# First attention of a fused transformer kernel: the scores of four heads as four row tiles of TensorE, in one set of PSUM banks, the values one step behind

## The chip, the cores and the metric

One Trainium2 chip; the kernel runs on one of its cores. The metric is the device time of one launch in microseconds. "Engines" are TensorE (PE; its weight loads are shown apart as PEld), VectorE (DVE), ScalarE (ACT), GpSimd (POOL) and SyncE (SP, which starts the transfers). PSUM has 8 banks of 128 partitions by 512 float32.

## The reference, cut to what matters

```python
x = L0_attn_x                                     # (1, 2048, 128)
x = x + _L0_attn_ref(_layernorm(x), w_qkv, w_proj, q_norm_w, k_norm_w)   # the first attention
x = x + _L0_ffn_ref(_layernorm(x), ...)           # a linear map by way of an FFT
x = x + _L1_attn_ref(_layernorm(x), ...)          # a linear attention
x = x + _L1_ffn_ref(_layernorm(x), ...)           # the second attention, 8 heads of 64, experts
# _L0_attn_ref: 16 heads of 8, causal, 2048 tokens
qkv = (x @ w_qkv.T).reshape(1, 2048, 3, 16, 8).transpose(2, 0, 3, 1, 4)
q, k = rope(rms_norm(q, q_norm_w)), rope(rms_norm(k, k_norm_w))
attn = jnp.einsum('bhqd,bhkd->bhqk', q, k) * 8 ** -0.5
attn = softmax(jnp.where(causal, -jnp.inf, attn), axis=-1)
out = jnp.einsum('bhqk,bhkd->bhqd', attn, v) ... @ w_proj.T
```

The change touches the first attention alone.

## The kernel before, in words

The tokens are 16 tiles of 128 (P); four tiles are a chunk of 512 (CH), and there are four chunks (NC). The 16 heads go in four groups (NG) of four (GH). In a group each head owns 32 partitions: `qT` holds the queries of the four heads under one another, and `kM[g % 2][:, h, :]` holds the keys of head h on partitions 32h to 32h+31 and zeros elsewhere. A matmul over all 128 partitions with `kM[.., h, ..]` as weights so gives the scores of head h alone.

**Foreground.** For a group there are 40 steps `STEPS0`, (c, jt) with query chunk c and key tile jt from 0 to 4c+3; over the four groups that is 160 steps k. In 96 of them the key tile lies before the chunk (jt < 4c, "off the diagonal": 512 queries), in 64 it lies on the diagonal (width 512, 384, 256 and 128 in turn, `off = diag(c, jt)`, and a second matmul adds the causal mask). For each step:
- S: the scores of the four heads, keys on partitions, into PSUM banks 0 to 3. Before, a unit u is two heads of a step (u = 2k, 2k+1), in banks 0, 1 or 2, 3; the unit waits until ACT has read the unit two before (`s_exp`, NS = 2).
- ACT takes the exponential of two banks at a time into `pbuf0` (line 976), two instructions a step.
- V: four matmuls, one for each head, as four column tiles (32 columns of weights each) into bank 6 (line 734), summed over the key tiles of a chunk. They are float32, and the trace shows two passes for each (8 a step). Before, V(k) is issued two steps behind S.
- O: after the last V of a chunk ACT copies bank 6 to `oT`; F: PE transposes it, DVE divides and stores it.

**Background.** Between them the preparation of the following chunks and group is woven in: transposes "k", "q", "q2" (line 667; ACT copies them out, "k" by four instructions of 32 partitions, line 963, "q" and "q2" by one, line 967), and "max" steps, in which PE computes scores with the queries on partitions (line 700, mask line 704) and DVE takes their maximum (line 1201, or line 1198 with a mask). The maximum goes into "q2" so that the exponentials don't overflow. These steps, and F and the later "at", "pj", "lt", "mix", "lin", share a ring of three banks, `RING0 = (4, 5, 7)`: in `take`, a step waits until the step three before it in the ring has been read out of its bank.

**The order.** One list, `SEQ0`, is followed by each engine. `preparation0` and `paced` give every background step a place on a scale of units (80 to a group); `merge` goes through the half units and puts, ahead of each, the background steps whose place has come, then what `foreground0(u, half)` returns. Before: S(u) at half 0 of each unit, V(k) (and O) at half 1 of unit 2k+4, F at half 1 of unit 2k+9. `after0` places the work that follows the last group.

Of the kernel before, what the change touches and what calls it, by code (L numbers as in the profile page):

```python
# [26 lines left out]
ACT = mybir.ActivationFunctionType  # L27
AX = mybir.AxisListType

P = 128  # L30
# [3 lines left out]
CH = 512  # L34
NC = T // CH
TPC = CH // P
H0, D0 = 16, 8
GH = 4
NG = H0 // GH
# [5 lines left out]
NP0, NP1 = 6, 5  # L45
NS = 2
# [152 lines left out]
def build(nc, A):  # L199
    ctx = ExitStack()  # L200
    with ctx:
# [6 lines left out]
        ps = ctx.enter_context(nc.psum_tensor("ps", [P, 8, CH], F32))  # L208
# [28 lines left out]
        identr = sm("identr", [P, P], F32R)  # L237
        maskr = sm("maskr", [P, 2, P], F32R)
# [22 lines left out]
        qT = s0("qT", [P, 2, T], F32R)  # L261
# [8 lines left out]
        pbuf0 = s0("pbuf0", [P, NP0, 2, CH])  # L270
# [20 lines left out]
        kM = (kM0, kM1)  # L291
# [71 lines left out]
        s_sc = sem("s_sc")  # L363
        s_exp = sem("s_exp")
        s_av = sem("s_av")
# [39 lines left out]
        STEPS0 = [(c, jt) for c in range(NC) for jt in range(TPC * (c + 1))]  # L405
        N0 = len(STEPS0)
        LAST0 = [TPC * (c + 1) * (c + 2) // 2 for c in range(NC)]
# [2 lines left out]


        def foreground0(u, half):
            if half == 0:
                return [("S", u)] if u < 2 * N0 * NG else []
            seq = []
            k = u // 2 - 2
            if u % 2 == 0 and 0 <= k < N0 * NG:
                seq.append(("V", k))
                if k % N0 + 1 in LAST0:
                    seq.append(("O", k // N0, LAST0.index(k % N0 + 1)))  # L420
            k = u // 2 - 4
            if u % 2 and 0 <= k < N0 * NG and k % N0 + 1 in LAST0:
                seq.append(("F", k // N0, LAST0.index(k % N0 + 1)))
            return seq

# [17 lines left out]

        after0 = []
        for c in range(NC):
            u = 2 * (N0 * (NG - 1) + LAST0[c] + 3) + 1
            for i, kind in enumerate(("at", "pj", "sd", "ln", "lt", "mix", "sd2", "ln2", "lt2")):
                after0.append((u + 1.8 + 1.6 * i, (kind, c)))
                if c == NC - 1 and kind in ("sd", "sd2"):
                    after0 += [(u + 2.0 + 1.6 * i, ("kv", b)) for b in ((0,) if kind == "sd" else (1, 2))]  # L450
            u += 1.8 + 1.6 * 9
            i = 3 * c
            for a, step in enumerate((("lin", i), ("lin", i + 1), ("ex", i), ("el", i), ("lin", i + 2), ("ex", i + 1),
                                      ("el", i + 1), ("ex", i + 2), ("el", i + 2))):
                after0.append((u + 0.8 * a, step))
# [31 lines left out]
        def diag(c, jt):  # L487
            return max(0, P * (jt - TPC * c))
# [89 lines left out]
        def _(sp):  # L578
# [24 lines left out]
                r = min(P, E1 * D1 - P * i)  # L603
                sp.dma_start(wout[0:r, i, :], A["Wo"][P * i:P * i + r, :]).then_inc(s_load1, 16)
            sp.dma_start(fold[:], A["fold"]).then_inc(s_load1, 16)
            sp.wait_ge(s_sc, 2 * N0 * NG)
            for h in range(H1):
                if h:
                    sp.wait_ge(s_wh, 3 * h)
# [13 lines left out]
        def _(pe):  # L623
# [54 lines left out]
            for step in SEQ0:  # L678
# [27 lines left out]
                                       start=False, stop=True, skip_group_check=True)  # L706
                    mm.then_inc(s_turn0, 1)
                elif kind == "S":
                    u = step[1]
                    g, (c, jt) = u // (2 * N0), STEPS0[u // 2 % N0]  # L710
                    off = diag(c, jt)
                    if u >= NS:
                        pe.wait_ge(s_exp, u - NS + 1)
                    wait_read(pe, ring0, ("q2", g, c))
                    wait_read(pe, ring0, ("k", g, c))
                    for i in range(2):
                        h = 2 * (u % 2) + i
                        b = 2 * (u % NS) + i
                        mm = pe.matmul(ps[:, b, off:CH], kM[g % 2][:, h, P * jt:P * (jt + 1)],  # L719
                                       qT[:, g % 2, CH * c + off:CH * (c + 1)], start=True, stop=jt < TPC * c)  # L720
                        if jt >= TPC * c:
                            mm = pe.matmul(ps[:, b, off:off + P], identr[:], maskr[:, 1, :], start=False, stop=True)  # L722
                    mm.then_inc(s_sc, 1)
                elif kind == "V":
                    k = step[1]
# [201 lines left out]
        def _(act):  # L927
# [22 lines left out]
            for step in SEQ0:  # L950
                kind = step[0]
                if kind in ("k", "q", "q2"):
                    _, g, c = step
                    wait_turn(act, ring0, step)
                    if g >= 2:
                        act.wait_ge(s_sc, 2 * N0 * (g - 1))
                    b = ring0.bank(step)
                    if kind == "k":
                        if g == 1:
# [7 lines left out]
                        nc.scalar.activation(qT[:, g % 2, CH * c:CH * (c + 1)], ps[:, b, :],  # L967
                                             ACT.Copy).then_inc(s_read0a, 1)
                elif kind == "S":
                    u = step[1]  # L970
                    off = diag(*STEPS0[u // 2 % N0])
                    act.wait_ge(s_sc, u + 1)
                    if u >= NP0:
                        act.wait_ge(s_av, (u - NP0) // 2 + 1)
                    b = 2 * (u % NS)
                    nc.scalar.activation(pbuf0[:, u % NP0, :, off:CH], ps[:, b:b + 2, off:CH], ACT.Exp,  # L976
                                         scale=float(D0) ** -0.5).then_inc(s_exp, 1)
                elif kind == "O":
                    _, g, c = step
                    m = g * NC + c  # L980
# [119 lines left out]
        def _(dve):  # L1100
# [61 lines left out]
            for step in SEQ0:  # L1162
# [74 lines left out]
                elif kind == "lin":  # L1237
                    i = step[1]
                    wait_turn(dve, ring0, step)
                    if i == 0:  # L1240
                        dve.wait_ge(s_stagev, NG)
                        dve.wait_ge(s_sc, 2 * N0 * (NG - 1))
                        dve.wait_ge(s_load1, 16 * 16)
                        v.memset(vf[:, :, D:D + 1], 1.0)
                        v.memset(vf[:, :, D + 1:D + 2], 0.0)
# [359 lines left out]
```

## Time and profile before

| | us |
|---|---|
| median of 3 runs | 1695.55 |
| lowest, highest | 1686.46, 1697.53 |
| profiled execution | 1687.58 |
| its span | 1685.8 |
| first attention in it, first to last step | 75.5 to 606.8 |

The profile comes from one execution. Busy times of PE are partly modelled (a matmul's end); starts are more reliable, so stretches on PE are read from start to start. An idle time in brackets stands before the instruction, with what ended it.

### The profile page before, as it was taken

What the parts mean: (1) busy time and instruction counts of PE and PEld (TensorE: products, weight loads), DVE (VectorE), ACT (ScalarE), POOL (GpSimd) and SP (SyncE); (2) the same over time, 40 slices, a digit from 0 to 9 for tenths busy, and PEclk for the clock granted to TensorE, in tenths of its full rate; (3) what the DMA queues carried; (4) which work ended last, traced back from release to release, by engine and by line L of the source; (5) the groups of instructions that cost most, each with busy time, mean ns of one, the idle gap of its engine ahead of it and who ended that gap; (6) DMA issues with size and microseconds to landing.
All of it is one profiled execution on the core that took longest, in us unless ns stands there. A gap on an engine that the chain in (4) does not pass through costs nothing.

```text
span 1685.8 us, 27140 instructions
## 1 busy us (share of the span) xinstructions
PE 1556.2 (92%) x8404; PEld 1012.7 (60%) x8404; DVE 1254.2 (74%) x2518; ACT 939.7 (56%) x1582; POOL 847.9 (50%) x935
## 2 busy tenths in 40 slices
PE   4699999999999976689999999999999999999998
PEld 2455565565565545466666666567576666666555
DVE  3997787687679536777887778787778787777664
ACT  3446756756755631344655655655655656556652
POOL 2530000000001133458869879788689699698452
PEclk9599999999999987989999999999999999999998
DMA  2000000000000000000000000000000000000000
GB/s 64 0 1 1 2 1 2 1 1 1 1 1 1 1 12 13 1 1 13 0 13 1 1 13 2 0 13 1 13 1 1 13 1 1 1 1 1 1 7 19
DMA packets 12230, 9.39 MB, mean 6 GB/s; under 512 B 3840, under 2 KB 11584, under 8 KB 12096
## 3 DMA queue, kind: packets, MB, share of 16 engines
q1 hardware_dynamic: 12096, 7.66, 1.7%
q8 instruction: 77, 1.26, 0.3%
q14 instruction: 57, 0.47, 0.1%
HBM read 6.61 MB, written 1.05 MB: 5 GB/s over the span
## 4 chain that ended last, share of the span: by engine, by line
PE 63%; POOL 18%; DVE 9%; issue 4%; ACT 4%; SPq 1%; DMA 0%; DVEq 0%; ACTq 0%; POOLq 0%
PE ps L887 10%; PE ps L700 9%; PE ps L734 7%; PE ps L719 7%; PE ps L860 5%; PE ps L875 5%; POOL gs L1526 4%; PE ps L667 4%; PE ps L876 4%; POOL gsum L1527 3%; POOL z L572 3%; POOL onm L566 3%; PE ps L898 2%; POOL h_qk L1528 2%; DVE mxp L1201 2%
## 5 line engine op out<-in xcount | busy, mean ns | idle before, releaser
L1080 ACT ACTIVATE pbuf<-ps 128x512 f32<-128x512 f32 x512 | 301.6, 599 | 170.4 <-PE ps L876 166.2
L976 ACT ACTIVATE pbuf<-ps 128x1024 f32<-128x1024 f32 (+3 forms) x320 | 280.1, 897 | 182.5 <-PE ps L722 92.2
L1201 DVE TENSOR_REDUCE mxp<-ps 128x1 f32<-128x512 f32 (+2 forms) x432 | 279.1, 685 | 82.8 <-PE ps L700 51.4
L1407 DVE TENSOR_TENSOR den<-den,pbuf 128x1024 f32<-128x1024 f32 x224 | 312.8, 1396 | 1.9
L887 PE MATMUL ps<-pbuf,h_v 128*64 128x512 f32 x1024 | 248.7, 606 | 0.0
L1066 ACT ACTIVATE relu<-ps 128x512 f32<-128x512 f32 x256 | 152.2, 599 | 161.2 <-PE ps L860 132.1
L1359 DVE TENSOR_TENSOR gt<-ps,gate 128x320 f32<-128x320 f32 x384 | 181.6, 483 | 78.4 <-POOL h_v L1536 36.4
L700 PE MATMUL ps<-kM,qT 128*128 128x512 f32 (+3 forms) x640 | 230.9, 414 | 9.2 <-ACT kM L963 4.9
L875 PE MATMUL ps<-q1T,k1T 128*128 128x512 f32 x512 | 215.3, 421 | 11.4 <-ACT pbuf L1080 9.9
L1380 DVE CUSTOM_DVE_ANT_0 relu<-ps,relu 128x512 f32<-128x512 f32 x256 | 174.2, 684 | 64.5 <-PE ps L860 61.7
L719 PE MATMUL ps<-qT,kM 128*128 128x512 f32 (+3 forms) x640 | 199.5, 381 | 8.5 <-ACT pbuf L976 8.5
L876 PE MATMUL ps<-q2T,k2T 65*128 65x512 f32 x512 | 203.8, 398 | 0.0
L700 PEld LDWEIGHTS ps<-kM,qT 128*128 128x128 f32 x640 | 115.5, 194 | 125.8 <-DVE mxp L1201 75.2
L566 POOL TENSOR_TENSOR onm<-on,topk 128x320 f32<-128x320 f32 x124 | 124.4, 1007 | 95.9 <-DVE on L1416 95.9
L572 POOL TENSOR_TENSOR z<-z,onm 128x320 f32<-128x320 f32 x124 | 160.7, 1301 | 0.0
L1526 POOL TENSOR_TENSOR gs<-gt 128x384 f32<-128x384 f32 x112 | 135.8, 1213 | 31.2 <-DVE gt L1359 31.2
L734 PE MATMUL ps<-pbuf,stagev 128*32 128x512 f32 (+3 forms) x1280 | 150.6, 543 | 0.0
L1469 POOL COPY stagev<-qkv 128x512 f32<-128x512 f32 x4 | 2.9, 722 | 278.9 <-PE ps L734 255.0
L719 PEld LDWEIGHTS ps<-qT,kM 128*128 128x128 f32 x640 | 117.7, 189 | 38.7 <-ACT pbuf L976 23.9
L842 PE MATMUL ps<-wh,xh 128*128 128x320 f32 x384 | 126.8, 330 | 13.2 <-DVE gt L1359 12.5
L887 PEld LDWEIGHTS ps<-pbuf,h_v 128*64 128x64 f32 x1024 | 62.3, 136 | 120.4 <-issue 97.9
L1454 POOL TENSOR_SCALAR rstd<-meanvar 128x4 f32<-128x4 f32 x12 | 2.7, 228 | 250.8 <-DVE meanvar L1115 250.8
(224 smaller groups left out, 2799.5 us busy)
## 6 DMA issues: line engine op xcount, KB each, us to landing
wraw<-in_Wkv SPq DMA_DIRECT2D x16, 160.0 KB, 2.5
wraw<-in_Wq SPq DMA_DIRECT2D x8, 160.0 KB, 2.3
out<-x SPq DMA_DIRECT2D x4, 256.0 KB, 2.3
wqkv<-in_wqkvT SPq DMA_DIRECT2D x1, 192.0 KB, 3.9
masks<-in_masks SPq DMA_DIRECT2D x1, 128.0 KB, 4.1
dft<-in_dft SPq DMA_DIRECT2D x1, 128.0 KB, 2.3
wout<-in_Wo SPq DMA_DIRECT2D x2, 64.0 KB, 2.6
ident<-in_ident SPq DMA_DIRECT2D x1, 64.0 KB, 5.8
```

The costliest lines, as they stand in the source:

```text
L572: eng.tensor_tensor(z[:, n], z[:, n], onm[:, i - 1], ALU.add).then_inc(s_z, 1)
L700: mm = pe.matmul(ps[:, bank, w * a:w * (a + 1)], qT[:, g % 2, P * it:P * (it + 1)], kM[g % 2][:, h + a, CH * b:CH * b + w], start=a == 0, ...
L719: mm = pe.matmul(ps[:, b, off:CH], kM[g % 2][:, h, P * jt:P * (jt + 1)], qT[:, g % 2, CH * c + off:CH * (c + 1)], start=True, stop=jt < TP ...
L734: mm = pe.matmul(ps[32 * h:32 * h + 32, ACC, off:CH], stagev[:, g % 2, jt, h, :], pbuf0[:, u % NP0, h % 2, off:CH], start=jt == 0, stop=jt ...
L875: pe.matmul(ps[:, i, :], k1T[h % 2][:, t], q1T[h % 2][:, q], start=True, stop=False)
L876: pe.matmul(ps[:, i, :], k2T[h % 2][0:D1 + 1, t], q2T[h % 2][0:D1 + 1, q], start=False, stop=True).then_inc(s_sc1, 1)
L887: mm = pe.matmul(ps[64 * i:64 * i + 64, ACC, :], h_v[:, h % 2, 2 * m + i, :], pbuf1[:, u % NP1, i, :], start=m == 0, stop=m == M1 - 1, til ...
L976: nc.scalar.activation(pbuf0[:, u % NP0, :, off:CH], ps[:, b:b + 2, off:CH], ACT.Exp, scale=float(D0) ** -0.5).then_inc(s_exp, 1)
L1080: nc.scalar.activation(pbuf1[:, u % NP1, i, :], ps[:, i, :], ACT.Exp, scale=float(D1) ** -0.5).then_inc(s_exp1, 1)
L1201: v.tensor_reduce(mxp[:, i, h:h + n, b], sc.rearrange("p (h k) -> p h k", h=n), AX.X, ALU.max).then_inc(s_read0d, 1)
L1407: v.tensor_tensor(dn, dn, w, ALU.add).then_inc(s_den1, 1)
L1526: link(g_.tensor_tensor(gs[:], t[:, :, 0:2, :], t[:, :, 2:4, :], ALU.add))
```

## The change

- `foreground0`: at half 0 of unit 2k come S(k), for all four heads, then V(k-1) and its O; nothing of the foreground stands at the three other half units of the step except F, at half 1 of unit 2k+5. The background steps keep their places.
- S(k) waits until ACT has taken all exponentials of S(k-1) (`s_exp` 2k): the four banks are one set.
- Off the diagonal the four matmuls use 32 partitions each, as four row tiles (`tile_position=(32 * h, 0)`), each into its own bank. On the diagonal the matmuls stay as they were, 128 partitions.
- ACT waits once for S(k), then issues both exponentials. Counts of `s_sc` are halved wherever they are waited for.
- `after0` begins four units earlier.

```diff
         def foreground0(u, half):
-            if half == 0:
-                return [("S", u)] if u < 2 * N0 * NG else []
             seq = []
+            k = u // 2
+            if (u % 2, half) == (0, 0):
+                if k < N0 * NG:
+                    seq.append(("S", k))
+                if 1 <= k <= N0 * NG:
+                    seq.append(("V", k - 1))
+                    if (k - 1) % N0 + 1 in LAST0:
+                        seq.append(("O", (k - 1) // N0, LAST0.index((k - 1) % N0 + 1)))
             k = u // 2 - 2
-            if u % 2 == 0 and 0 <= k < N0 * NG:
-                seq.append(("V", k))
-                if k % N0 + 1 in LAST0:
-                    seq.append(("O", k // N0, LAST0.index(k % N0 + 1)))
-            k = u // 2 - 4
-            if u % 2 and 0 <= k < N0 * NG and k % N0 + 1 in LAST0:
+            if (u % 2, half) == (1, 1) and 0 <= k < N0 * NG and k % N0 + 1 in LAST0:
                 seq.append(("F", k // N0, LAST0.index(k % N0 + 1)))
             return seq
...
-            u = 2 * (N0 * (NG - 1) + LAST0[c] + 3) + 1
+            u = 2 * (N0 * (NG - 1) + LAST0[c] + 1) + 1
...
                 elif kind == "S":
-                    u = step[1]
-                    g, (c, jt) = u // (2 * N0), STEPS0[u // 2 % N0]
+                    k = step[1]
+                    g, (c, jt) = k // N0, STEPS0[k % N0]
                     off = diag(c, jt)
-                    if u >= NS:
-                        pe.wait_ge(s_exp, u - NS + 1)
+                    if k:
+                        pe.wait_ge(s_exp, 2 * k)
                     wait_read(pe, ring0, ("q2", g, c))
                     wait_read(pe, ring0, ("k", g, c))
-                    for i in range(2):
-                        h = 2 * (u % 2) + i
-                        b = 2 * (u % NS) + i
-                        mm = pe.matmul(ps[:, b, off:CH], kM[g % 2][:, h, P * jt:P * (jt + 1)],
-                                       qT[:, g % 2, CH * c + off:CH * (c + 1)], start=True, stop=jt < TPC * c)
-                        if jt >= TPC * c:
-                            mm = pe.matmul(ps[:, b, off:off + P], identr[:], maskr[:, 1, :], start=False, stop=True)
+                    keys, queries = slice(P * jt, P * (jt + 1)), slice(CH * c + off, CH * (c + 1))
+                    for h in range(GH):
+                        if jt < TPC * c:
+                            rows = slice(32 * h, 32 * h + 32)
+                            mm = pe.matmul(ps[:, h, :], kM[g % 2][rows, h, keys], qT[rows, g % 2, queries],
+                                           start=True, stop=True, tile_position=(32 * h, 0))
+                        else:
+                            pe.matmul(ps[:, h, off:CH], kM[g % 2][:, h, keys], qT[:, g % 2, queries],
+                                      start=True, stop=False)
+                            mm = pe.matmul(ps[:, h, off:off + P], identr[:], maskr[:, 1, :], start=False, stop=True)
                     mm.then_inc(s_sc, 1)
...
                 elif kind == "S":
-                    u = step[1]
-                    off = diag(*STEPS0[u // 2 % N0])
-                    act.wait_ge(s_sc, u + 1)
-                    if u >= NP0:
-                        act.wait_ge(s_av, (u - NP0) // 2 + 1)
-                    b = 2 * (u % NS)
-                    nc.scalar.activation(pbuf0[:, u % NP0, :, off:CH], ps[:, b:b + 2, off:CH], ACT.Exp,
-                                         scale=float(D0) ** -0.5).then_inc(s_exp, 1)
+                    k = step[1]
+                    off = diag(*STEPS0[k % N0])
+                    act.wait_ge(s_sc, k + 1)
+                    if k >= NP0 // 2:
+                        act.wait_ge(s_av, k - NP0 // 2 + 1)
+                    for i in range(2):
+                        nc.scalar.activation(pbuf0[:, (2 * k + i) % NP0, :, off:CH], ps[:, 2 * i:2 * i + 2, off:CH],
+                                             ACT.Exp, scale=float(D0) ** -0.5).then_inc(s_exp, 1)
```

## Rows read from the trace of the kernel before

**Rows 1.** The page: the span.

```profile
span 1685.8 us, 27140 instructions
```

**Rows 2.** Busy time by stretch of the first attention: start:end, length, engines, granted clock.

```profile
75.50:156.40 80.90, 79.17 (x431) 46.09 (x430) 75.25 (x150) 39.92 (x47) 23.61 (x12) 1.00 0.00 1
221.40:350.40 129.00, 125.34 (x781) 76.16 (x780) 96.14 (x196) 84.31 (x109) 0.61 (x1) 0.99 0.00 1
478.20:561.40 83.20, 79.36 (x500) 49.51 (x498) 72.43 (x178) 46.07 (x59) 10.19 (x12) 1.00 0.00 1
561.40:606.80 45.40, 45.19 (x287) 22.95 (x285) 17.67 (x54) 34.32 (x46) 5.09 (x6) 1.00 0.01 1
```

**Rows 3.** Waits, 75.5 to 606.8 us: total, times, longest.

```profile
ACT pbuf L976 <- PE ps L722: 92.2, 88, 2.3
ACT pbuf L976 <- PE ps L719: 88.1, 95, 2.7
```

**Rows 4.** Groups of instructions, 75.5 to 606.8 us: busy, mean ns, idle before.

```profile
L976 ACT ACTIVATE pbuf<-ps 128x1024 f32<-128x1024 f32 (+3 forms) x320 | 280.1, 897 | 182.5 <-PE ps L722 92.2 <-PE ps L719 88.1
L1201 DVE TENSOR_REDUCE mxp<-ps 128x1 f32<-128x512 f32 (+2 forms) x421 | 272.2, 685 | 81.5 <-PE ps L700 50.7 <-PE ps L704 28.4
...
L719 PE MATMUL ps<-qT,kM 128*128 128x512 f32 (+3 forms) x640 | 199.5, 381 | 8.5 <-ACT pbuf L976 8.5
```

**Rows 5.** Timeline of one step off the diagonal: start, length, engine, line.

```profile
328.66 1.06 PE L734 MATMUL ps<-pbuf,stagev 128*32 128x512 f32 x8
...
329.66 0.50 PE L700 MATMUL ps<-kM,qT 128*128 128x512 f32 x1
...
329.99 0.63 PE L719 MATMUL ps<-qT,kM 128*128 128x512 f32 x2
330.19 0.70 DVE L1198 CUSTOM_DVE_ANT_0 ps<-ps,maskb 128x512 f32<-128x512 f32 x1 [0.39 <-PE ps L700]
...
330.46 0.62 PE L700 MATMUL ps<-kM,qT 128*128 128x512 f32 x2
330.66 1.94 ACT L976 ACTIVATE pbuf<-ps 128x1024 f32<-128x1024 f32 x2 [1.10 <-PE ps L719]
...
330.92 0.62 PE L719 MATMUL ps<-qT,kM 128*128 128x512 f32 x2
331.47 0.16 PEld L734 LDWEIGHTS ps<-pbuf,stagev 128*32 128x32 f32 x8 [0.36 <-issue]
```

**Rows 6.** Timeline, steps on the diagonal: widths 512 and 128, and a V of 384.

```profile
244.93 0.39 PE L719 MATMUL ps<-qT,kM 128*128 128x512 f32 x1
...
245.56 0.44 PE L700 MATMUL ps<-kM,qT 128*128 128x512 f32 x1
...
255.15 0.23 PE L719 MATMUL ps<-qT,kM 128*128 128x128 f32 x1
...
255.54 0.45 PE L700 MATMUL ps<-kM,qT 128*128 128x512 f32 x1
...
255.92 0.85 PE L734 MATMUL ps<-pbuf,stagev 128*32 128x384 f32 x8
...
256.70 0.50 PE L700 MATMUL ps<-kM,qT 128*128 128x512 f32 x1
```

**Rows 7.** Timeline, maxima in a row: DVE reads, and a wait of PE for one.

```profile
260.08 2.58 DVE L1201 TENSOR_REDUCE mxp<-ps 128x2 f32<-128x512 f32 x4 [0.28 <-PE ps L704]
...
97.64 0.91 PE L700 MATMUL ps<-kM,qT 128*128 128x512 f32 x3
...
98.03 0.30 PEld L700 LDWEIGHTS ps<-kM,qT 128*128 128x128 f32 x2 [0.41 <-DVE mxp L1201]
```

**Rows 8.** Timeline: ACT copies keys out, then PE waits for its exponential.

```profile
179.44 2.37 ACT L963 ACTIVATE kM<-ps 32x512 fp32r<-32x512 f32 x4
...
181.84 2.88 ACT L976 ACTIVATE pbuf<-ps 128x1024 f32<-128x1024 f32 x3
...
182.92 0.74 PE L719 MATMUL ps<-qT,kM 128*128 128x512 f32 x2
```

More of the change, by code:

```diff
@@ L605, in _ @@
             sp.dma_start(fold[:], A["fold"]).then_inc(s_load1, 16)
-            sp.wait_ge(s_sc, 2 * N0 * NG)
+            sp.wait_ge(s_sc, N0 * NG)
             for h in range(H1):
@@ L955, in _ @@
                     if g >= 2:
-                        act.wait_ge(s_sc, 2 * N0 * (g - 1))
+                        act.wait_ge(s_sc, N0 * (g - 1))
                     b = ring0.bank(step)
@@ L1241, in _ @@
                         dve.wait_ge(s_stagev, NG)
-                        dve.wait_ge(s_sc, 2 * N0 * (NG - 1))
+                        dve.wait_ge(s_sc, N0 * (NG - 1))
                         dve.wait_ge(s_load1, 16 * 16)
```

## The prediction

> **What bounds the kernel now.** I read the page for the span [rows 1], then the busy times by stretch, because the change touches only the first attention, 75.5 to 606.8 us. TensorE is busy 125.3 of 129.0 us in a middle group of heads, at full clock, and DVE 96.1 [rows 2]: TensorE sets the pace. Only in the first 81 us is DVE near its limit as well (75.3 of 80.9), and only the last 45 us have hardly any DVE work (17.7). The waits say the same from the other side: ACT stands waiting for scores of PE for 180 us in sum [rows 3], while PE's score matmuls waited for ACT only 8.5 us [rows 4].
>
> Next I took one step off the diagonal apart, from start to start [rows 5]. V: 328.66 to 329.66, 1.00 us. The first matmul behind it takes 0.33, later ones of 512 columns 0.23 each (0.47 for two), so 0.10 is a weight load that nothing hides when PE changes its tiling. The last score matmul starts at 331.15 and V at 331.47: 0.32, or 0.09 beyond its 0.23. By these parts a step with three maxima is 1.00 + 0.33 + 2 x 0.23 + 4 x 0.23 + 0.09 = 2.80; the row shows 2.81, so the parts can be trusted. With four maxima it is 3.03.
>
> **The change part by part.** *Scores off the diagonal.* Today they are four matmuls, 0.93 us. As row tiles they have no row. Bounds: all at once with nothing exposed, 0.21; as now one after another with a switch on both sides, 0.93 + 0.19 = 1.12. The nearest row is V, which is column tiled: eight matmuls of 512 columns take 1.00 us where eight at 0.23 would be 1.84, and their eight weight loads 0.16 [rows 5]. Tiles do run beside each other here. I take the exposed load 0.10, one matmul 0.23, 0.02 of issue and 0.09 to empty the array before V: 0.45. In between lies the case that tiles overlap but their 128-column loads follow each other by 0.10: 0.75. Gain per step 0.48; for 96 steps -46 us.
>
> The rows show tiles overlapping in V. The Trainium skill (TensorE: Matmul & The Clock Gate, Part 3) says that row tiles start some 4 ns apart and gives 3.07x for four of them at 512 columns; by that the scores would take 0.30 and the estimate would be 14 us lower. No run here shows row tiles yet.
>
> *The burst.* This is what I think decides. The order written by the background's places isn't changed, but the foreground no longer stands in between: all the background steps of a step k now follow each other behind V(k-1), then comes S(k+1). I counted them in the order that `preparation0` and `paced` give. Of the 143 steps k up to the end of the maxima, 127 have four or more steps of the ring (97 four, 17 five, 10 six, 1 seven, 2 eight). The ring has three banks. So the fourth of a burst waits until DVE has read the first. Price: first maximum starts, DVE begins 0.54 later (329.66 to 330.19, and it had been idle) [rows 5], reads 0.69 (mean) [rows 4], and a waiting PE starts 0.06 after its releaser (the exponential of about 1.02 that starts at 181.84 ends at 182.86, PE starts at 182.92) [rows 8]. Fourth start 1.29 after the first, against 0.33 + 0.23 + 0.23 = 0.79 unhindered: 0.50 of new idle time in each of the 127 steps, +63 us. That such waits exist where three maxima follow each other closely is in the trace, 0.41 at 98.03 [rows 7]. S(k+1) is queued behind the fourth on PE, and behind S(k+1) the exponentials. Every ring step beyond the fourth costs a DVE interval, (2.58 - 0.69) / 3 = 0.63 [rows 7], instead of 0.23: 48 such, +19. About 8 of these are paid today: the first stretch has 21 steps in 80.9 us [rows 2], where the parts on PE give about 73. So +11. F joins bursts instead of standing apart: 12 x 0.2, +3.
>
> A full step off the diagonal is then 1.00 + 1.29 + 0.32 + 0.45 = 3.06, against 3.03: gain and wait cancel. On the diagonal nothing is gained. A pair of scores at 512 takes 0.63, at 128 still 0.39 [rows 6], and V narrows too (0.78 at 384), but V's narrower steps only shift by one, so each step there pays the 0.50 plainly.
>
> *One set of banks.* S(k+1) waits for both exponentials of k, and they for S(k). Chain off the diagonal: two exponentials 1.94 [rows 5], 0.06, S until its result is there 0.10 + 0.02 + 0.39 + 0.04: 2.55 us. That is under 3.06, so it is covered by the burst; if the burst were shorter it would be the floor. In the last 17 steps, which have at most one background step, it is the pace: they take 45.4 us now [rows 2], 2.67 each; 12 at 2.55, and five on the diagonal with shorter exponentials but 0.8 to 1.3 of scores, about 12 in sum, make some 43. The first term took 6 off there, so +3.
>
> *ACT's other work.* Copies of 0.6 us fit into the 0.6 in which ACT waits for S. The keys' copies, 2.37 us [rows 8], don't: today the second set of banks lets PE go on. Three single ones 1.3 us each, three places with two in a row and their neighbours 2 each: +10. V(k-1) waits for the same exponentials that S(k) has waited for, nothing more; the next chunk's first V waits for the copy to `oT`, 0.6 us that S covers. SP's wait for `s_sc` stands at the end of the stage and keeps its meaning.
>
> *Credit.* PE is idle 3.7 us in a group [rows 2]; some of that coincides with the new waits: -8.
>
> **Sum:** -46 + 63 + 11 + 3 + 3 + 10 - 8 = +36. The profiled execution took 1687.6 (span 1685.8 [rows 1]), which gives 1724; the median of the runs is 8 above it and would give 1732. I take 1728.
>
> **The rivals.** *Gain and wait cancel* (within 17 us of before). If the scores take 0.25 as tiles, 84 steps gain 17 more; if half the credit I gave for idle time is too small, another 5. Sum about +12, 1707. For it: the 0.45 rests on no row of row tiles.
>
> *The burst doesn't hold* (faster). It needs the fourth ring step to start no later than 0.8 after the first, that is, DVE's read to be over by then; or S(k+1) to wait for ACT anyway so that both waits coincide. Then the terms 63 and 11 go, and the chain of exponentials becomes the floor: 2.55 off the diagonal, just what the parts give without the wait (2.56). -46 + 3 + 3 + 10 = -30, 1663. For it: DVE has 33 of 129 us spare in a middle group [rows 2]. Against it: spare time isn't the question, the delay of one matmul plus one read is.
>
> The Trainium skill (TensorEngine Tiling (Array Packing), PSUM Bottleneck) warns that after row tiling the reading of PSUM becomes the bound; here both readers would show it, DVE by the burst and ACT by the chain.
>
> *The tiles follow each other* (slower still). Loads 0.10 apart: 0.75 instead of 0.45, 84 x 0.30 = +25, 1753. Fully one after another: 1.12, +56, 1784. Against it: V's eight loads in 0.16.
>
> **How the numbers follow.** Two runs of this kernel differ by up to 0.7%, so 1% (17 us) is about what can be told from no change. Forecast (+18 to +50) 0.50; cancelled (within 17) 0.22; burst doesn't hold 0.12; tiles follow each other 0.16. Slower by over 1%: 0.66, same 0.22, faster 0.12. The range from 1692 to 1760 takes in the cancelled case's upper part, the forecast and the case of loads 0.10 apart; it leaves out the faster case, the rest of the cancelled one and fully serial tiles.
>
> **What the profile after would show.** Score matmuls off the diagonal: four starts within some 0.03 us, and 0.45 from their start to V's. The fourth PE background step behind each V: idle time of about 0.5 before it, ended by DVE's maxima (L1201 or L1198), in sum over 50 us. V to V 3.0 to 3.1 off the diagonal in a middle group, about 0.4 to 0.5 longer than now on it; a middle group some 136 instead of 129 us. PE's busy share in the stage falls under 85%. In the last 17 steps ACT's line 976 nearly without idle time but for the 0.6 of each step. Wrong I'd be if PE's clock fell for the idle pieces of 0.5 us (the stage has 1.00 now, with pieces of up to 2.9), if a background step's read ended sooner than the 1.23 I add up, or if PE took the scores of the tiles much more cheaply or dearly than V's rows suggest.

## The result and the profile after

The changed kernel takes 1752.76 us (median of 4 runs, 1745.81 to 1756.41); the kernel before, run beside it, 1695.91 (4 runs). The ratio is 1.034 with a 95% interval of 1.029 to 1.040: slower by 57 us, where I forecast 32. The profiled execution took 1755.66. The page of after:

```profile
span 1753.9 us, 26823 instructions
PE 1565.2 (89%) x8404; PEld 976.9 (56%) x8404; DVE 1247.2 (71%) x2518; ACT 934.0 (53%) x1582; POOL 847.9 (48%) x935
PEclk9799999999999996588999999999999999999999
```

The span grew by 68.1 us [rows 1]. From the first score matmul to the last V the stage went from 531.7 us to 590.1, so 58.4 of it lie there. All that follows took 1078.6 before and 1090.1 after, at a granted clock of 0.97 and 0.95. In the kernels measured below it took 1078 to 1079 where the clock was 0.97 and 1082 to 1088 where it was 0.96 or 0.95, with no relation to their edits; from here I go by the stage and by the medians. Medians below are over all runs; the ratios leave out two slow ones, one of e6 (1933.68 us at a granted clock of 0.73) and one of e5 (1702.20 us). Second, busy time by stretch, after; the stretches are bounded by the same score matmuls as in [rows 2] (first column start:end, then length, engines, granted clock):

```profile
73.60:170.80 97.20, 84.68 (x440) 42.06 (x438) 77.36 (x149) 38.40 (x47) 25.28 (x14) 0.96 0.00 1
242.65:383.31 140.66, 123.16 (x782) 63.51 (x781) 93.13 (x196) 83.18 (x108) 0.61 (x1) 0.99 0.00 1
524.70:616.90 92.20, 81.64 (x505) 44.25 (x504) 72.88 (x181) 45.44 (x60) 10.17 (x12) 1.00 0.00 1
616.90:663.70 46.80, 38.21 (x280) 16.82 (x278) 16.17 (x52) 33.51 (x45) 5.07 (x6) 0.96 0.01 1
```

Read the second line against [rows 2]. The middle group of heads is 11.7 us longer although PE is busy 2.2 us less: PE now stands idle for 17.5 of 140.7 us instead of 3.7 of 129.0. DVE (93.1) and ACT (83.2) have as much work as before. No engine is full, so a loop between engines sets the pace. The clock hardly moved in this group (0.99 in both). The first stretch is worse than the others in proportion (16.3 on 80.9), and its clock mean is 0.96; I come back to it.

Third, the waits of the stage (total, times, longest), and the group of the maxima's matmuls with the idle time before them:

```profile
ACT pbuf L980 <- PE ps L726: 126.7, 61, 7.0
PEld ps L701 <- DVE mxp L1205: 110.6, 177, 3.7
ACT pbuf L980 <- PE ps L721: 105.6, 73, 3.3
...
PEld ps L701 <- DVE mxp L1202: 30.4, 46, 0.8
```

```profile
L701 PE MATMUL ps<-kM,qT 128*128 128x512 f32 (+3 forms) x611 | 211.8, 425 | 40.1 <-DVE mxp L1205 24.9 <-DVE mxp L1202 5.6 <-ACT kM L967 3.5
```

ACT waits for PE 232 us where it was 180 [rows 3]: it has become less of a bound, not more. New is the matmul of the maxima (L701) waiting for DVE's reads. Whose idle time it is shows in one step. Fourth, the timeline of a step off the diagonal, after, to be held against [rows 5]:

```profile
297.55 0.51 PE L721 MATMUL ps<-qT,kM 32*128 32x512 f32 x4
...
297.98 1.06 PE L738 MATMUL ps<-pbuf,stagev 128*32 128x512 f32 x8
298.10 1.94 ACT L980 ACTIVATE pbuf<-ps 128x1024 f32<-128x1024 f32 x2 [1.16 <-PE ps L721]
...
298.98 0.85 PE L701 MATMUL ps<-kM,qT 128*128 128x384 f32 x3
299.46 0.57 DVE L1202 CUSTOM_DVE_ANT_0 ps<-ps,maskb 128x384 f32<-128x384 f32 x1 [0.70 <-PE ps L701]
...
300.13 0.19 PEld L701 LDWEIGHTS ps<-kM,qT 128*128 128x128 f32 x1 [0.69 <-DVE mxp L1202]
300.14 0.49 PE L701 MATMUL ps<-kM,qT 128*128 128x512 f32 x1 [0.31 <-DVE mxp L1202]
...
300.56 0.50 PE L721 MATMUL ps<-qT,kM 32*128 32x512 f32 x4
```

Four scores start at 297.55 and V starts at 297.98: 0.43 for a block that took 0.93. V takes its 1.00. Then three matmuls of the maxima run through, and the fourth stands before a bank that DVE hasn't read. A step on the diagonal, where there are no tiles to pay for it (timeline, after):

```profile
278.30 0.28 PE L724 MATMUL ps<-qT,kM 128*128 128x256 f32 x1
...
279.26 0.85 PE L738 MATMUL ps<-pbuf,stagev 128*32 128x384 f32 x8
279.37 1.08 ACT L980 ACTIVATE pbuf<-ps 128x512 f32<-128x512 f32 x2 [2.06 <-PE ps L726]
280.04 0.96 PE L701 MATMUL ps<-kM,qT 128*128 128x512 f32 x3
280.58 1.89 DVE L1205 TENSOR_REDUCE mxp<-ps 128x1 f32<-128x512 f32 x3 [0.88 <-PE ps L701]
...
281.33 0.50 PE L701 MATMUL ps<-kM,qT 128*128 128x512 f32 x1 [0.32 <-DVE mxp L1205]
...
281.67 0.22 PE L724 MATMUL ps<-qT,kM 128*128 128x128 f32 x1
```

From the first of the burst to the fourth 281.33 - 280.04 = 1.29 us. From the fourth to the next score 0.34, where the matmul itself is 0.23: its weight load waited with it, and nothing hides it.

The first stretch has one thing more. Timeline, after, 87.8 to 94:

```profile
87.87 1.87 POOL L558 TENSOR_TENSOR qkv<-qkv,tmp 128x768 f32<-128x768 f32 x1
...
88.23 3.31 DVE L1214 TENSOR_SCALAR stageq<-mx 128x16 fp32r<-128x16 f32 x1
89.68 1.82 POOL L559 TENSOR_TENSOR qkv<-qkv,tmp 128x768 f32<-128x768 f32 x1
91.45 3.07 DVE L1205 TENSOR_REDUCE mxp<-ps 128x1 f32<-128x512 f32 x5
...
92.18 1.39 PE L701 MATMUL ps<-kM,qT 128*128 128x512 f32 x2 [3.38 <-DVE mxp L1205]
```

A DVE write of 16 numbers per partition takes 3.31 us; the median of its 16 executions is 0.18. It ends at 91.54, GpSimd's second operation at 91.50. The ring stands behind it, PE is idle for 3.38 us, and in the window from 90 to 100 us the granted clock is 0.66, a mean of the two levels (1.2 and 2.4 GHz):

```profile
90.00:100.00 10.00, 7.82 (x35) 5.28 (x35) 6.68 (x10) 1.25 (x3) 9.04 (x3) 0.66 0.00 0
```

Before, the same window had 1.00.

This isn't the only place where the clock fell. In windows of 40 us it is 0.91 from 160 to 200 and 0.96 from 320 to 360, 440 to 480, 480 to 520 and 600 to 640. In the first three of them PE had just stood idle for 3.32 us, waiting for ACT's exponentials, which stood behind its copies of keys and queries (after: a window, start:end, length, engines, granted clock, and one such wait):

```profile
160.00:200.00 40.00, 32.70 (x200) 18.67 (x196) 20.42 (x51) 25.76 (x38) 0.00 (x0) 0.91 0.00 1
```

```profile
322.78 0.33 PE L724 MATMUL ps<-qT,kM 128*128 128x128 f32 x1 [3.32 <-ACT pbuf L980]
```

The kernel before has these idle pieces too, 2.61 to 2.86 us long, and its clock fell behind one of them (at 294). Over the whole stage the granted clock is 1.00 before and 0.98 after. If PE had had work all that time, the difference would be worth some 12 of the 58 us: an upper estimate, and no run separates it.

### The profile page after: what moved, and what is told of

Its sections match the earlier page's. It is cut to its first block, busy times and chain, and to the rows that moved or that the text cites. A ratio compares the mean times of both kernels' runs of the same rounds, so it can differ in the third digit from the quotient of the medians.

```text
span 1753.9 us, 26823 instructions
## 1 busy us (share of the span) xinstructions
PE 1565.2 (89%) x8404; PEld 976.9 (56%) x8404; DVE 1247.2 (71%) x2518; ACT 934.0 (53%) x1582; POOL 847.9 (48%) x935
## 4 chain that ended last, share of the span: by engine, by line
PE 57%; POOL 18%; DVE 14%; issue 5%; ACT 5%; SPq 1%; DMA 0%; DVEq 0%; ACTq 0%; POOLq 0%
PE ps L891 10%; PE ps L738 7%; PE ps L701 6%; DVE mxp L1205 5%; PE ps L864 5%; PE ps L879 4%; POOL gs L1530 4%; PE ps L668 4%; PE ps L880 4%; POOL gsum L1531 3%; POOL z L573 3%; POOL onm L567 3%; PE ps L724 3%; PE ps L721 2%; PE ps L902 2%
## 5 line engine op out<-in xcount | busy, mean ns | idle before, releaser
L980 ACT ACTIVATE pbuf<-ps 128x1024 f32<-128x1024 f32 (+3 forms) x320 | 269.4, 894 | 234.2 <-PE ps L726 126.7
L1205 DVE TENSOR_REDUCE mxp<-ps 128x1 f32<-128x512 f32 (+2 forms) x432 | 271.7, 682 | 123.5 <-PE ps L701 84.3
L701 PE MATMUL ps<-kM,qT 128*128 128x512 f32 (+3 forms) x640 | 223.4, 429 | 44.3 <-DVE mxp L1205 24.9
L701 PEld LDWEIGHTS ps<-kM,qT 128*128 128x128 f32 x640 | 109.2, 195 | 199.4 <-DVE mxp L1205 112.6
L848 PE MATMUL ps<-wh,xl 128*128 128x320 f32 x384 | 121.3, 316 | 0.0
L879 PEld LDWEIGHTS ps<-q1T,k1T 128*128 128x128 f32 x512 | 96.9, 189 | 42.9 <-ACT pbuf L1084 35.0
```

What stands on the lines that cost most here:

```text
L701: mm = pe.matmul(ps[:, bank, w * a:w * (a + 1)], qT[:, g % 2, P * it:P * (it + 1)], kM[g % 2][:, h + a, CH * b:CH * b + w], start=a == 0, ...
L879: pe.matmul(ps[:, i, :], k1T[h % 2][:, t], q1T[h % 2][:, q], start=True, stop=False)
L980: nc.scalar.activation(pbuf0[:, (2 * k + i) % NP0, :, off:CH], ps[:, 2 * i:2 * i + 2, off:CH], ACT.Exp, scale=float(D0) ** -0.5).then_inc( ...
L1205: v.tensor_reduce(mxp[:, i, h:h + n, b], sc.rearrange("p (h k) -> p h k", h=n), AX.X, ALU.max).then_inc(s_read0d, 1)
```

## The experiments

The theory of the prediction: tiles save some 46 us, the burst of four ring steps behind V costs some 60 and more, one set of score banks about 13. Rivals after the result: ACT's chain through the single set of banks is the bound; or the tiles saved less than they seem to.

**e1_v_between: take the burst apart.** V(k-1) goes between the two pairs of half slots again.

```diff
-            if (u % 2, half) == (0, 0):
-                if k < N0 * NG:
-                    seq.append(("S", k))
+            if (u % 2, half) == (0, 0) and k < N0 * NG:
+                seq.append(("S", k))
+            if (u % 2, half) == (1, 0):
                 if 1 <= k <= N0 * NG:
```

> The changed kernel with one thing moved: V(k-1) stands at half 0 of unit 2k+1, so that the background steps of a step k lie half before and half behind it; S(k) for four heads, row tiles and the one set of banks stay. Theory 1 (the burst of four background steps behind V waits for DVE through a ring of three banks): the wait of 0.5 us goes, one more change of tiling of 0.19 comes. A full step off the diagonal takes 0.44 + 0.65 + 1.00 + 0.65 = 2.74 instead of 3.0 to 3.1 (84 x -0.32 = -27), a step on the diagonal 0.3 to 0.4 less (-19), bursts of five and more some 0.4 less (-14): 60 us less than the changed kernel, about 1693, about as the kernel before. Idle time of PE before line 701 that DVE ended falls from over 50 us to under 15. Theory 2 (the one set of score banks costs the time: S waits for the exponentials, the exponentials for S): V's place doesn't matter, within 10 us of the changed kernel.

Measured: 1697.89 (10 runs), ratio to before 1.003 (1.000 to 1.006); the stage is 533.3 instead of 590.1, -56.8. The timeline of a step off the diagonal in it:

```profile
271.98 0.51 PE L721 MATMUL ps<-qT,kM 32*128 32x512 f32 x4
...
272.41 0.73 PE L701 MATMUL ps<-kM,qT 128*128 128x512 f32 x2
272.54 1.94 ACT L980 ACTIVATE pbuf<-ps 128x1024 f32<-128x1024 f32 x2 [0.71 <-PE ps L721]
...
273.07 1.06 PE L738 MATMUL ps<-pbuf,stagev 128*32 128x512 f32 x8
...
274.07 0.73 PE L701 MATMUL ps<-kM,qT 128*128 128x512 f32 x2
...
274.74 0.51 PE L721 MATMUL ps<-qT,kM 32*128 32x512 f32 x4
```

2.76 us from start to start and no wait of PE for DVE; the same four matmuls of maxima, in twos. The loss of the change is its order of work.

**e2_full_rows: the change without its row tiles.**

```diff
-                            rows = slice(32 * h, 32 * h + 32)
-                            mm = pe.matmul(ps[:, h, :], kM[g % 2][rows, h, keys], qT[rows, g % 2, queries],
-                                           start=True, stop=True, tile_position=(32 * h, 0))
+                            mm = pe.matmul(ps[:, h, :], kM[g % 2][:, h, keys], qT[:, g % 2, queries],
+                                           start=True, stop=True)
```

> The changed kernel without row tiles: off the diagonal the four score matmuls go over all 128 partitions again, everything else as changed. Theory 1: PE is in the chain through every step, so the 0.48 us that the tiles save in a step come back nearly in full: 84 to 96 times, +40 to +46 us, about 1796. Theory 2 (the exponentials and S follow each other, 2.55 us with tiles): the chain gets longer by the same 0.5, also +45, so this run doesn't tell 1 from 2. Theory 3 (DVE's reads of the maxima are the bound, PE's savings end as idle time): under +15.

Measured: 1798.84 (2 runs), ratio 1.060 (1.056 to 1.065); stage 635.5, so the tiles are worth 45.4 us in this order: 0.47 for each of the 96 steps.

**e3_half_reads: shorten DVE's part of the loop.** Each maximum reads half of its columns (so half of each maximum is left out); the matmuls stay.

```diff
-                        v.tensor_tensor_reduce(sc, sc, maskb[:, CH - w:CH], 1.0, ...
+                        v.tensor_tensor_reduce(sc[:, w // 2:w], sc[:, w // 2:w], maskb[:, CH - w // 2:CH], 1.0, ...
-                        v.tensor_reduce(mxp[:, i, h:h + n, b], sc.rearrange("p (h k) -> p h k", h=n),
+                        v.tensor_reduce(mxp[:, i, h:h + n, b], sc.rearrange("p (h k) -> p h k", h=n)[:, :, 0:w // 2],
```

> The changed kernel, but DVE takes each maximum over half of the columns (256 of 512), so part of the maximum that protects the exponential is left out. A read takes some 0.42 instead of 0.69 us. Theory 1: the fourth step of a burst waits 0.27 less, 127 times, and each further one 0.27 less, 48 times: -46 us, about 1707. Theory 2 (the chain of exponentials and scores): DVE's reads don't matter, within 10 us.

Measured: 1702.19 (8 runs), ratio 1.004 (1.001 to 1.007); stage 543.3, -46.8. Busy time of the same middle group in e3:

```profile
218.76:352.00 133.24, 123.54 (x781) 64.25 (x780) 58.24 (x196) 83.17 (x108) 0.61 (x1) 0.97 0.00 1
```

Here 35 us less DVE work shortened the group by 7.4 us, and that on an engine which had 47 of 141 us spare. What counts is how long one read is: 0.42 instead of 0.69. The fourth of a burst should now start after 0.54 + 0.42 + 0.06 = 1.02 instead of 1.29, and the timeline has 329.24 - 328.23 = 1.01:

```profile
328.23 1.51 PE L701 MATMUL ps<-kM,qT 128*128 128x512 f32 x4
328.76 1.44 DVE L1205 TENSOR_REDUCE mxp<-ps 128x1 f32<-128x256 f32 x4 [1.43 <-PE ps L701]
329.24 0.19 PEld L701 LDWEIGHTS ps<-kM,qT 128*128 128x128 f32 x1 [0.49 <-DVE mxp L1205]
```

An ordinary step becomes shorter by this much (2.88 against 3.13 at k = 98), a chunk's first step on the diagonal doesn't (3.50 against 3.52 at k = 100). That the stage as a whole loses just the 46 that I expected is in part luck: 18.7 of the 46.8 lie in the first stretch (97.2 to 78.5), where DVE was near its limit and its slow write took 1.53 instead of 3.31, and the later groups give 7 to 8 each.

**e4_act_longer: lengthen ACT's chain.** One more exponential per step, which reads a score bank into a buffer that nobody uses.

```diff
+        spare = s0("spare", [P, 2, 480], BF16)
...
+                    nc.scalar.activation(spare[:, k % 2, 0:min(480, CH - off)], ps[:, 0, max(off, 32):CH],
+                                         ACT.Exp, scale=float(D0) ** -0.5)
                     for i in range(2):
```

> The changed kernel with one more exponential in each step ahead of the two, of up to 480 columns of the first score bank, into a buffer that nobody reads; it adds some 0.45 us to ACT's part of each step. Theory 1: the chain of exponentials off the diagonal becomes 2.55 + 0.45 = 3.0, still under the 3.0 to 3.1 of the burst; only the last 17 steps (+7), the steps with few background steps (+5) and those with the keys' copies (+6) get longer: +18 us. Theory 2 (the chain sets the pace all through): 0.45 x 160 = +65 to +70 us.

Measured: 1771.92 (2 runs), ratio 1.045 (1.037 to 1.053); stage 606.1, +16.0. It lengthens ACT's chain by 0.46 us a step (the timeline of e4, where the second line is the pair of exponentials that the kernel needs):

```profile
299.67 0.57 ACT L980 ACTIVATE spare<-ps 128x480 bf16<-128x480 f32 x1 [0.73 <-PE ps L722]
300.13 1.93 ACT L983 ACTIVATE pbuf<-ps 128x1024 f32<-128x1024 f32 x2
```

Were the chain the bound, 160 steps would cost up to 74 us. In ordinary steps off the diagonal the time from start to start stays (3.14 and 3.15 at k = 97 and 98, against 3.14 and 3.13). It grows in each chunk's first step on the diagonal (4.05 against 3.52 at k = 100) and in the last 17 steps, where I had named the chain as the pace: 4.7 of the 16 us lie there, and the ordinary ones take 2.55 + 0.46 = 3.01. So the chain isn't what the ordinary steps of the middle wait for, but it isn't far away.

**e7_order_alone: the order without either of the rest.** The kernel before, with two sets of banks and full rows, in the order of after: both of its score steps together, then V one step behind.

```diff
+            k = u // 2
+            if (u % 2, half) == (0, 0):
+                if k < N0 * NG:
+                    seq += [("S", 2 * k), ("S", 2 * k + 1)]
+                if 1 <= k <= N0 * NG:
+                    seq.append(("V", k - 1))
...
-            u = 2 * (N0 * (NG - 1) + LAST0[c] + 3) + 1
+            u = 2 * (N0 * (NG - 1) + LAST0[c] + 1) + 1
```

> The kernel before with the order of the foreground alone: S(2k), S(2k+1), V(k-1) and O at half 0 of unit 2k, F and the last group's followers as in the changed kernel; no row tiles, two sets of banks as before. Theory 1: the burst is all there, the tiles' gain isn't, and the second set of banks spares only the last 17 steps (-8 against e2_full_rows), the keys' copies and the steps with few background steps (-8): about 1783, 86 us over the kernel before. Theory 2 (the one set of banks is what costs): near the kernel before, within 20 us.

Measured: 1781.11 (4 runs), ratio 1.052 (1.049 to 1.056); stage 617.8, +86.1. PE's timeline in it shows the burst with full rows:

```profile
303.58 1.06 PE L735 MATMUL ps<-pbuf,stagev 128*32 128x512 f32 x8
304.57 0.98 PE L701 MATMUL ps<-kM,qT 128*128 128x512 f32 x3
305.86 0.50 PE L701 MATMUL ps<-kM,qT 128*128 128x512 f32 x1 [0.31 <-DVE mxp L1202]
```

305.86 - 304.57 = 1.29 again. With e2 this splits the stage by differences of whole kernels: order +86.1 (e7 less before), one set of banks +17.7 (e2 less e7), row tiles -45.4 (after less e2). These sum to +58.4 by construction, each in the company in which it was measured. Of the 17.7, 8.2 lie in the last 17 steps (44.5 in e7, 52.7 in e2), where the exponentials wait for scores over full rows; with tiles, in after, these steps take 46.8.

**e8_old_rhythm: the change with the old places.** V(k-2) in slot (0, 1), F at `u // 2 - 4` and `after0` as before, with the tiles and one set of banks.

```diff
-                if 1 <= k <= N0 * NG:
-                    seq.append(("V", k - 1))
-                    ...
             k = u // 2 - 2
+            if (u % 2, half) == (0, 1) and 0 <= k < N0 * NG:
+                seq.append(("V", k))
...
+            k = u // 2 - 4
             if (u % 2, half) == (1, 1) and 0 <= k < N0 * NG and k % N0 + 1 in LAST0:
```

> The changed kernel with V, O, F and the followers at their old places (V two steps behind, at half 1 of unit 2k); row tiles and the one set of banks stay. One background step stands between S and V, three between V and the next S; the fourth ring step is then never less than 1.3 us behind the first. Theory 1: as good as e1_v_between, 1695 to 1700, although V is late again: what matters is that the burst is broken, not where. Theory 2: near the changed kernel.

Measured: 1706.33 (4 runs), ratio 1.009 (1.006 to 1.013); stage 546.1, 13 more than e1. Of this, 6 lie in the first stretch (87.4 against 81.4, with the slow DVE write at 3.17 us). What the other 7 are wasn't separated. So the old places aren't better for the new kernel; V between the pairs is.

**e6_f_later and e5_two_halves: what still holds e1 back.** Step by step against before, e1 is 0.3 us shorter in an ordinary step off the diagonal (2.75 against 3.04 at k = 97 to 98), and gives it back in a few others: the first, full-width step of each chunk's diagonal (3.50 against 2.96 at k = 100; 4.34 against 3.65 at k = 116) and the second step of a group (3.70 against 2.51 at k = 81). I took the step with F for another such place (3.20 against 2.41 at k = 85), but the kernel before has this F two steps later, at k = 87: from k = 84 to 87 e1 takes 11.50 and before 11.78. Besides, the granted clock of the stage is 0.98 in e1 and 1.00 before. The first kind is one set of banks, as this timeline of e1 shows:

```profile
349.81 0.40 PE L724 MATMUL ps<-qT,kM 128*128 128x512 f32 x1
...
351.14 0.68 PE L701 MATMUL ps<-kM,qT 128*128 128x512 f32 x2
351.75 0.43 PE L738 MATMUL ps<-pbuf,stagev 128*32 128x128 f32 x8
353.33 0.44 PE L724 MATMUL ps<-qT,kM 128*128 128x384 f32 x1 [0.46 <-ACT pbuf L980]
```

Four full-width scores with masks take 1.33 before the exponentials may begin, these take 1.94, and the next S waits for both: 3.52 from start to start, 0.46 of it idle. e6 moves F, and with it `after0`, one step later:

```diff
-            k = u // 2 - 2
+            k = u // 2 - 3
             if (u % 2, half) == (1, 1) and 0 <= k < N0 * NG and k % N0 + 1 in LAST0:
```

> As e1_v_between, with F and the work after the last group one step later (unit 2k+7). In e1 the PE stood 0.2 to 0.5 us ahead of each F, since V and with it the copy to oT come half a step later than in the changed kernel. With 16 of them: 4 to 8 us less than e1, about 1691. If what ends that idle time is not the copy but DVE, no gain.

Measured: 1695.52 (10 runs), ratio 1.000 (0.998 to 1.003); stage 536.1 against 533.3. The gain of 4 to 8 that I expected isn't there. The first stretch is 4.9 longer (86.3 against 81.4; the slow DVE write took 3.07 in e6 and 1.28 in e1), the rest 2.1 shorter. The cost of F moves with it (k = 85 and 86 together are 6.28 in e1, 6.21 in e5 with the same place for F as e6).

e5 adds to e6 that the score banks are handed over in halves: ACT may begin after two heads, and on the diagonal PE may write the first two banks after the first exponential. The other counts of `s_sc` are doubled.

```diff
-                        pe.wait_ge(s_exp, 2 * k)
+                        pe.wait_ge(s_exp, 2 * k if jt < TPC * c else 2 * k - 1)
...
+                        if h == 2 and k and jt >= TPC * c:
+                            pe.wait_ge(s_exp, 2 * k)
...
-                    mm.then_inc(s_sc, 1)
+                        if h % 2:
+                            mm.then_inc(s_sc, 1)
...
-                    act.wait_ge(s_sc, k + 1)
...
                     for i in range(2):
+                        act.wait_ge(s_sc, 2 * k + i + 1)
```

> As e6_f_later, and the scores are signalled and waited for in halves: on the diagonal the first two heads wait for the first exponential alone and the last two for the second, and ACT starts its first exponential when two heads are done. Where the chain of exponentials and scores sets the pace (about 20 of the 64 steps on the diagonal, those with few background steps or of width 512) a step gets some 0.4 us shorter, and ACT gets to the keys' copies earlier: 5 to 12 us less than e6_f_later, about 1683. If the one set of banks never was in the way once V is moved: no difference from e6_f_later.

Measured: 1693.38 (10 runs), ratio 0.998 (0.995 to 1.002); stage 526.3, 9.8 less than e6. The same step in e5:

```profile
346.92 0.40 PE L726 MATMUL ps<-qT,kM 128*128 128x512 f32 x1
...
349.81 0.34 PE L726 MATMUL ps<-qT,kM 128*128 128x384 f32 x1
```

2.89 instead of 3.52. Of the 9.8 us only about half belong to the hand-over: 4.9 lie in the first stretch, where e5's slow write took 1.28 instead of 3.07. In the rest of the stage the hand-over in halves is worth 4.9 (444.9 against 449.8); in the medians it is no more than a tendency.

**e9_after_no_lock, e11_before_no_lock: the slow write.** The negated copy of the maxima is written by a reduction over an axis of one element instead of `tensor_scalar`, in after (e9) and in before (e11).

```diff
-                    v.tensor_scalar(stageq[:, TPC * c:TPC * (c + 1), :, 24:25].bitcast(F32R), mx[:].unsqueeze(3),
-                                    -1.0, None, ALU.mult).then_inc(s_m, 1)
+                    v.tensor_reduce(stageq[:, TPC * c:TPC * (c + 1), :, 24].bitcast(F32R), mx[:].unsqueeze(3),
+                                    AX.X, ALU.max, negate=True).then_inc(s_m, 1)
```

> The changed kernel with the small write of the negated maxima (line 1214, a TENSOR_SCALAR of 16 values) done as a TENSOR_REDUCE. In the changed kernel's profile this write took 2.48 us at 66.4 and 3.31 us at 88.2, where GpSimd was rotating the other heads, and 0.18 us everywhere else; behind the second PE stood still for 3.4 us and its clock was 0.66 for the next 10 us. If the tensor_scalar is held up by GpSimd's instructions and a reduce is not: both take about 0.2 us, 2.3 + 3.1 us less, and some 2 us of clock: 5 to 8 us under the changed kernel, about 1746. If the write itself has to wait for something else there (a semaphore, the link before it), the long times stay.

> The kernel before with the same write as a TENSOR_REDUCE; it took 2.51 and 0.84 us there. 2 to 3 us less than before, about 1693: within what can be told from no change. It shows how much of e10_best is owed to this write.

This line of after, and of e9 (durations are min/median/max in ns), and the window from 90 to 100 us of e9:

```profile
L1214 DVE TENSOR_SCALAR stageq<-mx x16: 181/182/3312, 66.3 to 615.5; 128x16 fp32r<-128x16 f32 x16
```

```profile
L1214 DVE TENSOR_REDUCE stageq<-mx x16: 179/182/186, 65.6 to 614.1; 128x16 fp32r<-128x16 f32 x16
```

```profile
90.00:100.00 10.00, 9.23 (x62) 4.69 (x60) 8.21 (x15) 5.63 (x8) 8.37 (x3) 1.00 0.00 0
```

The long execution is gone, and in this window the clock stays up. The first stretch of e9 is 91.6 instead of 97.2, but the two middle groups are 143.2 and 142.4 instead of 140.7 and 141.4, and the stage falls only from 590.1 to 588.0. Its granted clock is 0.97 where after has 0.98: in the later groups it was low for longer. The medians agree: 1750.61 (6 runs), ratio 1.032 (1.028 to 1.036). In before nothing is gained that can be told: 1693.09 (12 runs), ratio 0.998 (0.995 to 1.000), stage 531.7 as without it.

**e10_best: e5 with that write.**

> e5_two_halves (V between the background steps, F later, scores handed over in halves, row tiles) with the same write as a TENSOR_REDUCE. There the write took 2.50 and 1.28 us. 2.3 + 1.1 us less than e5_two_halves: about 1690, 0.3 to 0.6% under the kernel before, if that can be told from it at all.

Measured: 1681.67 (12 runs, 1678.07 to 1698.15), ratio 0.994 (0.991 to 0.997), stage 525.9. Faster than both kernels: by 0.6% against before, and some 4% against after. Its middle group, beside that of after above:

```profile
223.25:349.39 126.14, 120.08 (x782) 63.32 (x781) 94.76 (x196) 83.51 (x108) 0.62 (x1) 0.97 0.00 1
```

PE is idle 6.1 us of 126.1; after had 17.5 of 140.7. The stage is 5.8 us under before's. The medians differ by more than that, and which part of the rest belongs to the edit isn't settled.

## Why the prediction was right, and where it was off

Forecast slower by 32 us within 1692 to 1760; it is slower by 57, near the upper end. The mechanism is the one that I named, but the sum was too small: the stage's +58.4 stands against +36. That 1753 is also the time of the rival with loads 0.10 apart is chance; its mechanism didn't occur.

- *Scores off the diagonal, -46.* Right: 0.45 assumed, 0.43 to 0.44 measured, -45.4 by e2. The four starts lie within 0.01 us. So the rival of tiles that follow each other (0.75 or 1.12) falls. So does the one of full cancellation as far as it hoped for 0.25. The Trainium skill (TensorE: Matmul & The Clock Gate, Part 3) gives 3.07x for four row tiles; by that figure the 0.93 would become an estimate of 0.30. The trace doesn't agree: the measured 0.43 to 0.44 is 2.1 to 2.2x, but it includes the change of tiling on both sides, which the figure doesn't price.
- *The wait of the fourth, 0.50.* Right: first to fourth 1.29 as worked out, in after and in e7. e3 confirms the parts by changing one of them: with reads of 0.42 it is 1.01. The sign that I named for it came out smaller: I expected over 50 us of idle time before these matmuls, and the rows have 40.1, of which DVE ended 30.5. PE's rows draw a matmul longer than the 0.23 to the next start, so a wait of 0.50 between starts shows there as 0.32.
- *The order as a whole, 63 + 11 + 3 - 8 = 69.* Mis-sized; e7 measures 86. A step of the working was missing: I let the fourth matmul cost its 0.23 and the next score start as if nothing had been held up. But its weight load waits for the same bank. From its start to the next score it is 0.34 instead of 0.23 in front of full rows, and 300.56 - 300.14 = 0.42 instead of 0.32 in front of tiles. 127 x 0.11 = 14 us of the 17 missing. F in a burst costs 0.65 to 0.7 instead of the 0.2 that I took, 12 times, +6, and for the credit of 8 nothing in the traces speaks. These make 28 where 17 are missing, so the 11 for further steps of the ring may have been too much. Against that stands the clock, for which the sum has no term: it is 0.98 in the stage of e7 and 1.00 before, worth up to some 10 us. No run separates these smaller terms.
- *One set of banks, 3 + 10 = 13.* 18 by e2 less e7, but 8 of these lie in the last 17 steps and come from full rows, as said above. The forecast saw the copies of the keys, but had each chunk's first diagonal step as covered. Four full-width scores and then two exponentials are 3.5 there in e1. In after it is the same 3.52 at k = 100, against 2.99 in e7 with two sets; at k = 116 it lies partly under the burst (4.35 against 4.08). At the copies, PE's idle pieces are 3.32 us in after and 2.83 in e7.
- *The chain of 2.55 as the pace of the last 17 steps.* Right: in after such steps start at 624.84, 627.39 and 629.94, 2.55 apart, and e4 lengthens this stretch by 4.7 us. But the stretch takes 46.8, not some 43: two steps, k = 149 and 150, took 3.11 and 3.77, and the granted clock of the stretch is 0.96.
- *The clock.* I had said I would be wrong if it fell for idle pieces of 0.5 us. A middle group full of them has 0.99, as before. But I had taken 1.00 for the whole stage, and it is 0.98: the clock fell in six places, three of them right behind an idle piece of 3.32 us at the copies, one behind the 3.38 of the slow write. e9 takes the last away and 2 us go. What the others cost isn't measured; 12 us of the 58 is the most.
- *Busy share and group.* PE's busy share of the stage is 87%, not under 85%, and the middle group takes 140.7, not 136.
- *"The burst doesn't hold"* was the faster rival. As a forecast of after it is wrong. Nor is its 1663 what a kernel without the burst takes: e1 is 1698. The terms that it left, -46 and +16, aren't all that remains; the ordinary steps take 2.76 instead of the 2.55 of the chain, and the diagonal's first steps, the second step of each group and the lower clock take back what the tiles gain. How e1's remainder divides between these I only read from its steps; it isn't measured by an edit of its own, but for the 4.9 us of e5.
- *Two slips of arithmetic.* 36 - 17 - 5 is 14, not 12, and from the start that gives 1728 for +36, -30 gives 1662, not 1663. Neither moves a chance.

## What to carry to other kernels

Where several producers' steps share a ring of buffers, count how many of them stand next to each other in the order of the engine that fills it: in a burst one longer than the ring the last step can't start sooner after the first than the delay to the reader plus one read, whatever the reader's busy share, and here the waiting matmul's weight load came on top (0.34 instead of 0.23). A long wait has a second price if the clock falls behind it, so the granted clock of the whole stage belongs into the comparison and not only that of its middle. Saving time on an engine isn't worth moving other work out from between such steps; here the tiles saved 45 us and closing up the order cost 86. Measure a change of three parts as three kernels: the sum told nothing of a part worth keeping.

## What the runs showed of the hardware

A DVE `tensor_scalar` of 128x16 took 2.49 and 3.31 us in after instead of 0.18 when it started beside GpSimd's operations on two operands (0.48 to 3.23 in the other kernels that have it); the longest ended within 0.05 us of one of them (91.54 and 91.50). The same write as a `tensor_reduce` took 0.18 at the same place (e9, e10, e11). The Trainium skill (SBUF — State Buffer, Who interferes with whom) says that DVE and GpSimd share a port pair as an exclusive lock, that `tensor_scalar` may take it and `tensor_reduce` never does on trn2; the traces agree in both halves. On the critical path of before it cost nothing that could be measured.

Four matmuls of 32 rows and 512 columns on four row tiles, into four banks, started within 0.01 us of each other and took 0.43 us to the start of V, the change of tiling before V included.
